# Counting the ones of a graph's adjacency: a column of the attention products against a pass over the stored mask in the second layer

## The chip, the cores and the metric

The kernel runs on one core of one Trainium2 chip. The metric is the device time of one execution in microseconds (us), the median over several executions. TensorE is PE in the profile, its weight loads PEld, VectorE is DVE, ScalarE is ACT, GpSimd is POOL and SyncE, which here only issues DMAs, is SP. L894 is line 894 of the kernel before.

## What is computed

Two graph layers over 8192 nodes with 128 features and a dense 8192 x 8192 adjacency of zeros and ones in float32 (256 MB). Cut to what matters:

```
h = relu(layernorm(x));  Wh = h @ W
e = leaky_relu(Wh @ a1 + (Wh @ a2).T, 0.2)          # 8192 x 8192
att = softmax(where(adj > 0, e, -9e15), axis=1)
x = x + GRU(att @ Wh, h)                            # first layer
h = relu(layernorm(x))
x = x + adj @ (h @ W1.T + b1)                       # second layer
```

The fast path of the kernel is right only if every element of the adjacency is 0 or 1, so it also tests that: for each strip of rows it counts the elements that are not zero and the elements that are exactly one, and if the two counts differ anywhere, a slow general path is run afterwards. With these inputs the counts agree and that path isn't run. The change concerns where the ones are counted.

## The kernel before

**The first layer.** The adjacency is read once, as 128 transposed pieces of 2 MB: 32 blocks of 256 nodes (`NS = 32`, index `g`) times 4 chunks (`CS = 4`, index `c`), each chunk holding 16 groups of 128 neighbours (`JC = 16`). For each piece VectorE writes `Y`, a fp8 mask that is 0.5 where the element equals one (`ones_of`, L617), which SP stores to HBM (`mask_bytes`, 512 KB a piece) for the second layer. The leaky ReLU's two slopes split the mask in two: ScalarE (L469) and VectorE (L672) compute the sign of the edge value for the groups of 128, and VectorE makes the two masks by a bitwise AND (L680) and XOR (L684) into `M`. ScalarE counts the elements that are not zero: a sign of the raw words, summed along the row (`count`, L478, and L556 for four pieces that are counted late).

TensorE then multiplies each mask (the weights, fp8, 128 x 128) with a table `TB` (the moving side, f16), 256 products a block and 8192 in all (`products`, L894). A row of the table has 129 high parts (128 features and the softmax denominator), 129 low parts, and before the change a column of ones, which makes each product 259 columns wide and counts the elements of the mask. ScalarE copies the four sums of a block out (`evacuate`, L490), VectorE adds high and low parts (`attended`, L689) and the two counts (L690, into `cn`), and a GRU and a layer norm follow for the block, spread over the next three blocks' slots. The result of a block is a row of `GS`, the 256 f16 columns (128 high, 128 low) that the second layer multiplies with.

**The second layer.** For each of the 32 strips `t` the whole stored mask of 2 MB is loaded (`y_load`, L313) into one of four buffers: the two `X` buffers and two pieces of the space of `TB`. TensorE makes 128 products of 256 columns a strip (`span`, L977), VectorE adds the two halves and the residual (`finish`, L797 and L802), and SP stores the strip (L320) and loads the next residual (L316). TensorE orders its work as: most of strips 0, 1 and 2 between the last steps of the GRU, then the rest of these three, then strip 3 and on, one after the other (`rest`). `rest(t)` waits for its strip's mask (`q_in`) and for strip t-4 to be finished (`q_o`). SP's loop loads strip t after TensorE is through with strip t-4 (`q_pe`), then waits for `q_o` and stores.

**The late counting.** Four of the 128 pieces are counted only after the last attention product: ScalarE issues their loads into `Z`, two buffers in the space of `M` (L562), and counts each as it lands (L556). VectorE meanwhile runs `examine` (two long reductions over `GS`, L807 and L808, and small ones) and then the `finish` steps. The counts are joined in `tally`, summed over partitions by TensorE (L1023), and the verdict is made in `judge`.

The queues are strictly in order on each engine, and the semaphore `c_cnt` counts ScalarE's counting passes (128 in all before).

Of the kernel before, what the change touches and what calls it, by code (L numbers as in the profile page):

```python
# [5 lines left out]
N = 8192  # L6
F = 128
P = 128
NT = N // P
# [58 lines left out]
def binary_adjacency(nc, sem, redo, xb, adjb, w, wt, a, wiht, whht, b_ih, b_hh, w1t, b1, out):  # L68
    ctx = ExitStack()
    with ctx:  # L70
# [45 lines left out]
        nz = sb("nz", [P, NS, CS])  # L116
        cn = sb("cn", [P, NT])
        den = sb("den", [P, NT])
# [16 lines left out]
        junk = JK[:, 0:JC * RW // 4].bitcast(u8)  # L135
        Mf = M[:, :, :].rearrange("p c k -> p (c k)").bitcast(f32)
        Z = [Mf[:, b * JC * RW:(b + 1) * JC * RW] for b in range(2)]

# [46 lines left out]
        t_p, t_hi, t_lo, t_lop = sem("t_p"), sem("t_hi"), sem("t_lo"), sem("t_lop")  # L185
        t_sc = k_w = sem("t_sc")

        c_in = [sem(f"c_in{b}") for b in range(2)]
# [47 lines left out]
        with nc.Block() as block:  # L236
            @block.sync
            def _(sp):
# [98 lines left out]
                with sp.Fori(1, NS // 4) as k:  # L337
                    for b in range(4):
                        sp.wait_ge(q_pe, k * 4 + b - 3)
                        y_load(k * 4 + b, b)  # L340
                        sp.wait_ge(q_o, k * 4 + b - 3)
                        store(k * 4 + b - 4, b % 2)
                        x1_load(k * 4 + b - 2, b % 2)
# [9 lines left out]
            def _(pool):  # L353
# [13 lines left out]
                for k in range(3):  # L367
                    pool.wait_ge(p_bias, 2 * k + 1)
                    nc.gpsimd.tensor_copy(bpart[k], src[k]).then_inc(p_bias, 1)
                    if k < 2:  # L370
                        pool.wait_ge(p_bias, 2 * k + 2)
                        nc.gpsimd.tensor_tensor(bres[k], src[k], bpart[k], ALU.subtract).then_inc(p_bias, 1)
                pool.wait_ge(b_in, 112)
                nc.gpsimd.memset(TB[:, :, :, 2 * TW:2 * TW + 2], 1.0).then_inc(p_one, 1)

# [17 lines left out]
            def _(act):  # L393
# [57 lines left out]
                def table_high(i):  # L451
                    act.wait_ge(t_p, i + 1)
                    if i == 0:
                        act.wait_ge(p_one, 3)
                    j, m = i // 2 * 8, i % 2
                    nc.scalar.activation(TB[:, j:j + 8, m, 0:TW], PB[i % 2], ACT.Copy).then_inc(t_hi, 1)
# [25 lines left out]
                def evacuate(q):  # L482
                    for t in range(2):
                        if t == 0:
                            act.wait_ge(e_t0, q + 1)
                        else:
                            act.wait_ge(c_pe, (q + 1) * CS)
                        wait(act, d_hp, q)
                        for m in range(2):
                            ins = nc.scalar.activation(AE[:, 2 * t + m, 0:2 * TW + 1], A[t][m][:, 0:2 * TW + 1], ACT.Copy)  # L490
                        ins.then_inc(e_ev[t], 1)
# [59 lines left out]
                for n in range(LATE + 2):  # L551
                    if n >= 2:
                        g, c = late[n - 2]
                        act.wait_ge(c_in[n % 2], (NS * 2 + n // 2) * 16)
                        act.wait_ge(c_cnt, (NS - 1) * EARLY + n - 2)
                        nc.scalar.activation(junk, Z[n % 2].bitcast(u32), ACT.Sign,  # L556
                                             accum_out=nz[:, g:g + 1, c:c + 1].rearrange("p g c -> p (g c)")).then_inc(
                                                 c_cnt, 1)
                        act.wait_ge(c_cnt, (NS - 1) * EARLY + n - 1)
                    if n < LATE:  # L560
                        g, c = late[n]
                        act.dma_start(Z[n % 2], adjb[g * CS + c, :, :]).then_inc(c_in[n % 2], 16)  # L562

            @block.vector
            def _(dve):
# [120 lines left out]
                def attended(q):  # L686
                    for t in range(2):
                        dve.wait_ge(e_ev[t], q + 1)
                    nc.vector.tensor_tensor(AE[:, :, 0:TW], AE[:, :, 0:TW], AE[:, :, TW:2 * TW], ALU.add).then_inc(d_sum, 1)  # L689
                    nc.vector.tensor_tensor(cn[:, bass.ts(q, 2)],  # L690
                                            AE[:, 0:4:2, 2 * TW:2 * TW + 1].rearrange("p t f -> p (t f)"),
                                            AE[:, 1:4:2, 2 * TW:2 * TW + 1].rearrange("p t f -> p (t f)"), ALU.add)
                    dve.wait_ge(d_sum, q + 1)
# [93 lines left out]
                for g in range(NS, NS + 3):  # L787
                    slot(g, g % 2, g // 2)

                def finish(t, u, b, n):  # L790
                    sums = PH2[b][:, :].rearrange("p (t f) -> p t f", f=2 * F)
# [13 lines left out]
                def examine():  # L805
# [3 lines left out]
                    nc.vector.tensor_reduce(bad[:, 2:3], den[:, :], AX.X, ALU.min).then_inc(k_v, 1)  # L809
                    nc.vector.tensor_reduce(odd[:, :, 1:2], cn[:, :].rearrange("p (g t) -> p g t", t=2), AX.X,  # L810
                                            ALU.add).then_inc(k_v, 1)
                    nc.vector.tensor_tensor(bad[:, 5:6], kt[:, 2:3], bad[:, 5:6], ALU.subtract).then_inc(k_v, 1)
                    nc.vector.tensor_tensor(tmp[:, 0, :], wext[:, 2:F + 2], wext[:, 2:F + 2], ALU.mult).then_inc(k_df, 1)
                    dve.wait_ge(k_v, 5)
                    nc.vector.scalar_tensor_tensor(bad[:, 0:1], bad[:, 1:2], -1.0, bad[:, 0:1], ALU.mult,
                                                   ALU.max).then_inc(k_v, 1)

                def tally():
                    dve.wait_ge(c_cnt, NS * CS)
                    nc.vector.tensor_reduce(odd[:, :, 0:1], nz[:, :, :], AX.X, ALU.add).then_inc(k_df, 1)  # L820
                    dve.wait_ge(k_df, 2)
                    nc.vector.scalar_tensor_tensor(odd[:, :, 0:1], odd[:, :, 1:2], -1.0 / MARK, odd[:, :, 0:1], ALU.mult,
                                                   ALU.add).then_inc(k_df, 1)

                def judge():
# [6 lines left out]
                    for n, (at, limit, op) in enumerate(limits):  # L832
                        dve.wait_ge(k_v, 9 + n)
                        nc.vector.scalar_tensor_tensor(bad[:, 7:8], bad[:, at:at + 1], limit, bad[:, 7:8], op,
                                                       ALU.mult).then_inc(k_v, 1)
                    dve.wait_ge(k_v, 14)
                    nc.vector.tensor_scalar(bad[:, 7:8], bad[:, 7:8], 0.5, None, ALU.is_lt).then_inc(k_v, 1)

                examine()
                for b in range(4):  # L840
                    finish(b, b % 2, b, b // 2)
                with dve.Fori(1, NS // 4 - 1) as k:
                    for b in range(4):
                        finish(k * 4 + b, b % 2, b, k * 2 + b // 2)
                tally()
                for t in range(NS - 4, NS):
                    finish(t, t % 2, t % 4, t // 2)
                    if t == NS - 3:
                        judge()
                dve.wait_ge(k_all, 1)  # L850
# [5 lines left out]
            def _(pe):  # L856
# [34 lines left out]
                def products(g, c, t):  # L891
                    for jj in range(JC):
                        for m in range(2):
                            ins = nc.tensor.matmul(A[t][m][:, 0:2 * TW + 1],  # L894
                                                   rows((mask1, mask2)[m](c), jj)[:, t * P:(t + 1) * P],
                                                   TB[:, c * JC + jj, m, 0:2 * TW + 1], start=(c == 0 and jj == 0),
                                                   stop=(c == CS - 1 and jj == JC - 1))
                    return ins
# [55 lines left out]
                def slot(g, u, k):  # L954
                    for c in range(CS):
                        if isinstance(g, int) and g == 0:
                            pe.wait_ge(t_lo, 2 * (c + 1))
                            pe.wait_ge(t_lop, 2 * (c + 1))
                            if c == 0:
                                pe.wait_ge(p_one, 3)  # L960
                        pe.wait_ge(c_m2, g * CS + c + 1)
# [40 lines left out]
                for b in range(3):  # L1002
                    for d in range(2):
                        ins = span(b, b, d, early, NT)
                    ins.then_inc(q_pe, 1)

                def rest(t, b, n):
                    pe.wait_ge(q_in[b], (n + 1) * 16)
                    wait(pe, q_o, t - 3)
                    pe.sem_inc(turn, 1)  # L1010
                    for d in range(2):
                        ins = span(t, b, d, 0, NT)
                    ins.then_inc(q_pe, 1)

# [4 lines left out]
                for t in range(NS - 4, NS):  # L1019
                    rest(t, t % 4, t // 4)  # L1020
                    if t == NS - 4:
                        pe.wait_ge(k_df, 3)
                        nc.tensor.matmul(GP[:, 0:NS], ones[:, :], odd[:, :, 0:1].rearrange("p g o -> p (g o)"), start=True,  # L1023
                                         stop=True)
                        nc.tensor.matmul(GP[:, P:2 * P], ones[:, :], tmp[:, 0, :], start=True, stop=True).then_inc(k_w, 1)
                pe.wait_ge(k_v, 15)
                nc.tensor.matmul(TG[0:1, 0:1], bad[:, 7:8], ones[:, 0:1], start=True, stop=True).then_inc(k_all, 1)
# [660 lines left out]
```

## Time and profile before

| | |
|---|---|
| median of 3 runs | 1615.08 us (1614.78 to 1615.68) |
| the profiled execution, own time | 1614.28 us |
| its span, first to last instruction | 1612.7 us |
| mean granted TensorE clock over the span | 0.984 |
| PE busy | 1536.0 us (95%) |
| DVE busy | 1138.4 us (71%) |
| ACT busy | 1065.8 us (66%) |
| PE products of the first layer, L894 | 8192, from 70 us to 1152 us |
| PE products of the second layer, L977 | 4096, from 1152 us to 1604 us |

Each engine's busy time is a share of the whole span, but the kernel has two long stages that load the engines differently. In the first layer PE, DVE and ACT are all busy over 95% of the time; in the second, from about 1222 us, DVE runs under 1 us in each 14 us and ACT nothing at all. The 1.6 us between the span and the execution's own time are start and end.

### The profile page before, as it was taken

The page shows a single profiled execution, that of the slowest core. Times are in us where ns is not written, and L with a number is a line of the kernel's source. Part 1 is how long each engine was busy: PE and PEld are TensorE (multiplying, and loading weights), DVE is VectorE, ACT ScalarE, POOL GpSimd, SP SyncE. Part 2 cuts the span into 40 slices and gives each one's busy share as a digit, 9 for nine tenths or more (in the row PEclk, how much of TensorE's full clock was granted, in tenths as well). Part 3 has the DMA queues.
Part 4 walks back from the last instruction along what each step waited for, and adds up shares of the span by engine and source line. Part 5 has one row for each costly group of instructions (what it writes and reads, how often), then busy time and mean ns, then how long its engine had stood idle before and what let it go on. Part 6 is the DMA issues. An engine that isn't in the chain of part 4 may idle for free.

```text
span 1612.7 us, 34927 instructions
## 1 busy us (share of the span) xinstructions
PE 1536.0 (95%) x13260; PEld 1335.1 (83%) x13260; DVE 1138.4 (71%) x2290; ACT 1065.8 (66%) x1805; POOL 44.5 (3%) x59
## 2 busy tenths in 40 slices
PE   5448999999999999999999999999999999999997
PEld 5336888888888888888888888888888888888887
DVE  8799999999999999999999999999250000000001
ACT  5669999999999999999999999999121000000000
POOL 0220000000000000000000000000000000000000
PEclk9779999999999999999999999999999999999999
DMA  8649999999999999999999999997558444444430
GB/s 330 237 153 348 340 341 338 339 345 336 339 343 339 340 337 344 340 344 338 340 344 341 343 331 341 342 337 283 212 214 357 174 162 159 161 165 176 176 124 15
DMA packets 79955, 454.16 MB, mean 282 GB/s; under 512 B 9176, under 2 KB 38434, under 8 KB 58914
## 3 DMA queue, kind: packets, MB, share of 16 engines
q1 hardware_dynamic: 78322, 444.54, 74.6%
q10 hardware_dynamic: 1584, 8.98, 1.4%
q8 instruction: 28, 0.46, 0.1%
q14 instruction: 21, 0.17, 0.0%
HBM read 369.57 MB, written 83.92 MB: 281 GB/s over the span
## 4 chain that ended last, share of the span: by engine, by line
PE 92%; DVE 5%; DMA 1%; issue 1%; ACT 0%; DVEq 0%; ACTq 0%
PE A L894 56%; PE A L977 28%; PE GP L918 3%; PE GP L919 2%; DMA h_columns<-AE 1%; PE GQ L937 1%; DVE AE L653 1%; PE GP L920 1%; PE GP L917 1%; DVE M L672 1%; DVE JK L653 1%; DVE Y L617 1%; PE TG L904 0%; PE TG L926 0%; DVE JK L569 0%
## 5 line engine op out<-in xcount | busy, mean ns | idle before, releaser
L894 PE MATMUL A<-TB,M 128*128 128x259 f16 x8192 | 940.8, 275 | 47.1 <-DVE M L684 41.1
L894 PEld LDWEIGHTS A<-TB,M 128*128 128x128 fp8e4 x8192 | 797.4, 97 | 174.0 <-issue 48.3
L469 ACT ACTIVATE M<-SB,dsteep 128x256 fp8e4<-128x256 f32 x1164 | 477.5, 502 | 0.0
L478 ACT ACTIVATE JK<-X 128x4096 uint8<-128x4096 uint32 x124 | 448.0, 3613 | 0.0
L617 DVE TENSOR_SCALAR Y<-X 128x4096 fp8e4<-128x4096 f32 x128 | 292.7, 2287 | 3.8 <-DMA X<-in_adjb_dram 3.7
L797 DVE SCALAR_TENSOR_TENSOR hp<-A,R 128x256 f32<-128x256 f32 x32 | 13.6, 425 | 367.5 <-PE A L977 349.0
L672 DVE TENSOR_SCALAR M<-SB,nd 128x256 fp8e4<-128x256 f32 x884 | 250.2, 355 | 0.0
L977 PE MATMUL A<-WG,X 128*128 128x256 f16 x2048 | 225.7, 273 | 0.0
L977 PE MATMUL A<-WG,TB 128*128 128x256 f16 x2048 | 225.2, 273 | 0.0
L977 PEld LDWEIGHTS A<-WG,TB 128*128 128x128 fp8e4 x2048 | 200.4, 98 | 23.2
L977 PEld LDWEIGHTS A<-WG,X 128*128 128x128 fp8e4 x2048 | 200.4, 98 | 23.1
L684 DVE TENSOR_TENSOR M<-Y,M 128x1024 uint32<-128x1024 uint32 x128 | 156.8, 1225 | 4.4
L680 DVE TENSOR_TENSOR M<-M,Y 128x1024 uint32<-128x1024 uint32 x128 | 155.9, 1218 | 0.5 <-issue 0.4
L490 ACT ACTIVATE AE<-A 128x259 f32<-128x259 f32 x128 | 42.0, 383 | 43.3 <-PE A L894 43.3
L918 PE MATMUL GP<-wihT,hpT 128*128 128x384 f32 x128 | 51.7, 486 | 0.0
L386 POOL TENSOR_TENSOR rstd<-ve,half 128x2 f32<-128x2 f32 x32 | 22.9, 716 | 1041.8 <-DVE ve L741 1041.8
L919 PEld LDWEIGHTS GP<-whhT,R 128*128 128x128 f32 x128 | 24.3, 190 | 17.0
L919 PE MATMUL GP<-whhT,R 128*128 128x256 f32 x128 | 38.1, 379 | 0.0
L689 DVE TENSOR_TENSOR AE<-AE 128x516 f32<-128x516 f32 x32 | 22.4, 699 | 21.8 <-ACT AE L490 21.6
L920 PEld LDWEIGHTS GP<-whhT,R 128*128 128x128 f32 x128 | 24.3, 190 | 3.3
L918 PEld LDWEIGHTS GP<-wihT,hpT 128*128 128x128 f32 x128 | 24.3, 190 | 2.4
L556 ACT ACTIVATE JK<-M 128x4096 uint8<-128x4096 uint32 x4 | 14.5, 3617 | 17.9 <-DMA M<-in_adjb_dram 17.9
(133 smaller groups left out, 696.8 us busy)
## 6 DMA issues: line engine op xcount, KB each, us to landing
X<-in_adjb_dram SPq DMA_DIRECT2D x128, 2048.0 KB, 9.5
mask_bytes<-Y SPq DMA_DIRECT2D x128, 512.0 KB, 4.7
X<-mask_bytes SPq DMA_DIRECT2D x16, 2048.0 KB, 9.3
TB<-mask_bytes SPq DMA_DIRECT2D x16, 2048.0 KB, 9.2
M<-in_adjb_dram ACTq DMA_DIRECT2D x4, 2048.0 KB, 10.2
M<-in_xb_dram SPq DMA_DIRECT2D x8, 512.0 KB, 8.5
h_rows<-M SPq DMA_DIRECT2D x8, 512.0 KB, 6.6
R<-in_xb_dram SPq DMA_DIRECT2D x32, 128.0 KB, 6.8
```

The costliest lines, as they stand in the source:

```text
L469: ins = nc.scalar.activation(rows(mask1(c), jj), SB[u][:, :], ACT.Sigmoid, scale=STEEP, bias=dsteep[:, j:j + 1], saturate=False)
L478: nc.scalar.activation(junk, X[c % 2][:, :].bitcast(u32), ACT.Sign, accum_out=nz[:, bass.ts(g, 1), c:c + 1].rearrange("p g c -> p (g c)")) ...
L490: ins = nc.scalar.activation(AE[:, 2 * t + m, 0:2 * TW + 1], A[t][m][:, 0:2 * TW + 1], ACT.Copy)
L617: nc.vector.tensor_scalar(Y[c % 2][:, :].bitcast(f8), X[c % 2][:, :], 1.0, MARK, ALU.is_equal, ALU.mult, saturate=False).then_inc(c_y, 1)
L672: ins = nc.vector.tensor_scalar(rows(mask1(c), jj), SB[u][:, :], nd[:, j:j + 1], None, ALU.is_ge, saturate=False)
L680: nc.vector.tensor_tensor(mask1(c), mask1(c), Y[c % 2][:, :], ALU.bitwise_and).then_inc(c_m1, 1)
L684: nc.vector.tensor_tensor(mask2(c), Y[c % 2][:, :], mask1(c), ALU.bitwise_xor).then_inc(c_m2, 1)
L894: ins = nc.tensor.matmul(A[t][m][:, 0:2 * TW + 1], rows((mask1, mask2)[m](c), jj)[:, t * P:(t + 1) * P], TB[:, c * JC + jj, m, 0:2 * TW + ...
L918: nc.tensor.matmul(bank[:, 0:3 * F], a_t, wihT[:, :], start=False, stop=False)
L919: nc.tensor.matmul(bank[:, 0:2 * F], h_t, whhT[:, 0:2 * F], start=False, stop=False)
L920: ins = nc.tensor.matmul(bank[:, 3 * F:4 * F], h_t, whhT[:, 2 * F:3 * F], start=False, stop=True)
L977: ins = nc.tensor.matmul(PH2[b][:, d * 2 * F:(d + 1) * 2 * F], YB[b][:, j * RW + d * P:j * RW + (d + 1) * P], GS[:, j, :], start=(d == 0 a ...
```

## The change

The table's rows lose the column of ones: the 8192 attention products are 258 columns wide, the copies out of PSUM too, and the addition into `cn` is gone, as is GpSimd's writing of the ones. The ones are counted from the stored mask in the second layer: for each strip VectorE adds the two halves of the 16384 fp8 values of a partition into 8192 (`halved`), and ScalarE sums these with its accumulator into `cy`. The halves lie in the space of `M` that the late loads (`Z`) use, so the first `halved` waits for all 128 counting passes. `halved(t)` stands ahead of `finish(t)` in VectorE's queue. Since the mask buffer of a strip is now also read by VectorE, SP loads strip t after `q_o` of strip t-4, not after `q_pe`. `tally`, `judge` and TensorE's small sums move to the last strip.

```diff
-        cn = sb("cn", [P, NT])
+        cy = sb("cy", [P, NS])
+        halves = [Mf[:, b * N // 4:(b + 1) * N // 4].bitcast(f8) for b in range(2)]
+        junk8 = Mf[:, N // 2:3 * N // 4].bitcast(u8)
...
                 with sp.Fori(1, NS // 4) as k:
                     for b in range(4):
-                        sp.wait_ge(q_pe, k * 4 + b - 3)
+                        sp.wait_ge(q_o, k * 4 + b - 3)
                         y_load(k * 4 + b, b)
-                        sp.wait_ge(q_o, k * 4 + b - 3)
                         store(k * 4 + b - 4, b % 2)
                         x1_load(k * 4 + b - 2, b % 2)
...
-                            ins = nc.scalar.activation(AE[:, 2 * t + m, 0:2 * TW + 1], A[t][m][:, 0:2 * TW + 1], ACT.Copy)
+                            ins = nc.scalar.activation(AE[:, 2 * t + m, 0:2 * TW], A[t][m][:, 0:2 * TW], ACT.Copy)
...
+                for t in range(NS):
+                    act.wait_ge(q_half, 16 + t + 1)
+                    act.wait_ge(c_cnt, NS * CS + t)
+                    nc.scalar.activation(junk8, halves[t % 2], ACT.Copy, accum_out=cy[:, t:t + 1]).then_inc(c_cnt, 1)
...
-                    nc.vector.tensor_tensor(cn[:, bass.ts(q, 2)],
...
+                def halved(t, b, n):
+                    dve.wait_ge(q_in[b], (n + 1) * 16)
+                    dve.wait_ge(c_cnt, NS * CS + (max(t - 1, 0) if isinstance(t, int) else t - 1))
+                    dve.sem_inc(turn, 1)
+                    nc.vector.tensor_tensor(halves[b % 2], YB[b][:, 0:N], YB[b][:, N:2 * N], ALU.add,
+                                            saturate=False).then_inc(q_half, 1)
...
                 examine()
                 for b in range(4):
+                    halved(b, b, 0)
                     finish(b, b % 2, b, b // 2)
                 with dve.Fori(1, NS // 4 - 1) as k:
                     for b in range(4):
+                        halved(k * 4 + b, b, k)
                         finish(k * 4 + b, b % 2, b, k * 2 + b // 2)
+                halved(NS - 4, 0, NS // 4 - 1)
+                for t in range(NS - 4, NS - 1):
+                    halved(t + 1, t % 4 + 1, NS // 4 - 1)
+                    finish(t, t % 2, t % 4, t // 2)
                 tally()
-                for t in range(NS - 4, NS):
-                    finish(t, t % 2, t % 4, t // 2)
-                    if t == NS - 3:
-                        judge()
+                judge()
+                finish(NS - 1, 1, 3, (NS - 1) // 2)
...
-                            ins = nc.tensor.matmul(A[t][m][:, 0:2 * TW + 1],
+                            ins = nc.tensor.matmul(A[t][m][:, 0:2 * TW],
                                                    rows((mask1, mask2)[m](c), jj)[:, t * P:(t + 1) * P],
-                                                   TB[:, c * JC + jj, m, 0:2 * TW + 1], start=(c == 0 and jj == 0),
+                                                   TB[:, c * JC + jj, m, 0:2 * TW], start=(c == 0 and jj == 0),
```

VectorE's queue at the start of the second layer, from the end of `examine` on, before the change. A00 to A11 are the PSUM banks of strips 0 to 3, R holds the residual and the result.

```order
L815 SCALAR_TENSOR_TENSOR bad<-bad 128x1 [waits k_v]
L797 SCALAR_TENSOR_TENSOR hp<-A00,R 128x256 [waits q_x0,q_pe]
L802 SCALAR_TENSOR_TENSOR R<-A00,hp 128x256 [waits q_lo]
L797 SCALAR_TENSOR_TENSOR hp<-A01,R 128x256 [waits q_x1,q_o,q_pe]
L802 SCALAR_TENSOR_TENSOR R<-A01,hp 128x256 [waits q_lo]
```

The same place after the change.

```order
L822 SCALAR_TENSOR_TENSOR bad<-bad 128x1 [waits k_v]
L796 TENSOR_TENSOR M<-X0 128x8192 [waits q_in0,c_cnt]
L806 SCALAR_TENSOR_TENSOR hp<-A00,R 128x256 [waits q_x0,q_pe]
L811 SCALAR_TENSOR_TENSOR R<-A00,hp 128x256 [waits q_lo]
L796 TENSOR_TENSOR M<-X1 128x8192 [waits q_in1,c_cnt]
L806 SCALAR_TENSOR_TENSOR hp<-A01,R 128x256 [waits q_x1,q_o,q_pe]
L811 SCALAR_TENSOR_TENSOR R<-A01,hp 128x256 [waits q_lo]
```

A pass over the strip's mask that waits for `c_cnt` now stands ahead of each pair of `finish` instructions.

SP's queue at the first turn of the second layer's loop, before the change. X0 receives strip 4, X1 strip 5.

```order
L313 ISA [waits q_pe]
L313 DMA X0<-mask_bytes 128x4096
L320 ISA [waits q_o]
L320 DMA out_0_dram<-R 128x256
L316 ISA
L316 DMA R<-x_after_gat 128x256
L313 ISA [waits q_pe]
L313 DMA X1<-mask_bytes 128x4096
```

The same place after the change.

```order
L316 ISA [waits q_o]
L316 DMA X0<-mask_bytes 128x4096
L323 ISA
L323 DMA out_0_dram<-R 128x256
L319 ISA
L319 DMA R<-x_after_gat 128x256
L316 ISA [waits q_o]
L316 DMA X1<-mask_bytes 128x4096
```

The load of a strip's mask stands behind the wait for `q_o`, which `finish` raises, where it stood behind TensorE's `q_pe`.

## Rows read from the trace of the kernel before

**Rows 1.** The page: busy time and share of each engine; the chain.

```profile
PE 1536.0 (95%) x13260; PEld 1335.1 (83%) x13260; DVE 1138.4 (71%) x2290; ACT 1065.8 (66%) x1805; POOL 44.5 (3%) x59
...
PE 92%; DVE 5%; DMA 1%; issue 1%; ACT 0%; DVEq 0%; ACTq 0%
PE A L894 56%; PE A L977 28%; PE GP L918 3%; PE GP L919 2%; DMA h_columns<-AE 1%; PE GQ L937 1%; DVE AE L653 1%; PE GP L920 1%; PE GP L917 1%; DVE M L672 1%; DVE JK L653 1%; DVE Y L617 1%; PE TG L904 0%; PE TG L926 0%; DVE JK L569 0%
```

**Rows 2.** The chain in order of time, first layer: start us, us, what.

```profile
416.08 7.16 PE A L894 x64
...
423.91 14.32 PE A L894 x128
```

**Rows 3.** The same view, second layer.

```profile
1188.53 373.57 PE A L977 x3422
...
1562.54 41.93 PE A L977 x384
```

**Rows 4.** The same view, before the first layer: f32 products of 130 columns.

```profile
20.20 0.89 PE A L867 x8
```

**Rows 5.** Waits in 60:160 us: who <- whom, total, times, longest.

```profile
PE A L894 <- DVE M L684: 41.1, 4, 18.7
...
PE A L894 <- issue: 6.0, 1, 6.0
```

**Rows 6.** Windows: busy us (instructions) of each engine, PEclk, DMA share, GB/s.

```profile
400.00:800.00 400.00, 400.00 (x3423) 344.21 (x3422) 387.41 (x760) 385.35 (x647) 8.68 (x12) 1.00 0.92 340
```

**Rows 7.** Waits in 400:800 us, 12.2 blocks.

```profile
ACT AE L490 <- PE A L894: 14.7, 12, 1.2
DVE AE L689 <- ACT AE L490: 5.4, 10, 0.6
```

**Rows 8.** Groups by line and form: busy us, mean ns, idle before.

```profile
L478 ACT ACTIVATE JK<-X 128x4096 uint8<-128x4096 uint32 x124 | 448.0, 3613 | 0.0
L617 DVE TENSOR_SCALAR Y<-X 128x4096 fp8e4<-128x4096 f32 x128 | 292.7, 2287 | 3.8 <-DMA X<-in_adjb_dram 3.7
...
L684 DVE TENSOR_TENSOR M<-Y,M 128x1024 uint32<-128x1024 uint32 x128 | 156.8, 1225 | 4.4
...
L690 DVE TENSOR_TENSOR cn<-AE 128x2 f32 x26 | 4.0, 154 | 0.0
...
L807 DVE TENSOR_REDUCE bad<-WG 128x1 f32<-128x8192 f16 x1 | 8.7, 8677 | 0.0
```

**Rows 9.** Timeline around the late counting: start us, us, instruction.

```profile
1196.34 0.34 SPq L313 DMA_DIRECT2D X<-mask_bytes  x1
...
1201.18 0.34 ACTq L562 DMA_DIRECT2D M<-in_adjb_dram  x1
...
1207.10 0.42 DVE L797 SCALAR_TENSOR_TENSOR hp<-A,R 128x256 f32<-128x256 f32 x1
1207.55 0.42 DVE L802 SCALAR_TENSOR_TENSOR R<-A,hp 128x256 f32<-128x256 f32 x1
...
1208.16 0.36 SPq L320 DMA_DIRECT2D out_dram<-R  x1
...
1208.53 0.33 ACTq L562 DMA_DIRECT2D M<-in_adjb_dram  x1
...
1212.18 3.62 ACT L556 ACTIVATE JK<-M 128x4096 uint8<-128x4096 uint32 x1 [3.68 <-DMA M<-in_adjb_dram]
...
1212.49 27.94 PEld L977 LDWEIGHTS A<-WG,X 128*128 128x128 fp8e4 x256
...
1217.93 3.62 ACT L556 ACTIVATE JK<-M 128x4096 uint8<-128x4096 uint32 x1 [2.04 <-DMA M<-in_adjb_dram]
```

**Rows 10.** The page: DMA issues, KB each, median us to landing.

```profile
X<-mask_bytes SPq DMA_DIRECT2D x16, 2048.0 KB, 9.3
```

**Rows 11.** The chain in order of time: 64 products after a wait of PE.

```profile
120.03 9.57 PE A L894 x64
135.57 8.66 PE A L894 x64
```

**Rows 12.** Windows over the same two stretches.

```profile
120.00:129.40 9.40, 9.37 (x64) 0.75 0.86 293
135.50:144.00 8.50, 8.43 (x64) 0.83 0.98 379
```

More of the change, by code:

```diff
@@ L186, in binary_adjacency @@
         t_sc = k_w = sem("t_sc")
+        q_half = t_p
         c_in = [sem(f"c_in{b}") for b in range(2)]
@@ L372, in _ @@
                         nc.gpsimd.tensor_tensor(bres[k], src[k], bpart[k], ALU.subtract).then_inc(p_bias, 1)
-                pool.wait_ge(b_in, 112)
-                nc.gpsimd.memset(TB[:, :, :, 2 * TW:2 * TW + 2], 1.0).then_inc(p_one, 1)
                 for i in range(1, 16, 2):
@@ L453, in table_high @@
                     if i == 0:
-                        act.wait_ge(p_one, 3)
+                        act.wait_ge(b_in, 112)
                     j, m = i // 2 * 8, i % 2
@@ L689, in attended @@
                     nc.vector.tensor_tensor(AE[:, :, 0:TW], AE[:, :, 0:TW], AE[:, :, TW:2 * TW], ALU.add).then_inc(d_sum, 1)
-                    nc.vector.tensor_tensor(cn[:, bass.ts(q, 2)],
-                                            AE[:, 0:4:2, 2 * TW:2 * TW + 1].rearrange("p t f -> p (t f)"),
-                                            AE[:, 1:4:2, 2 * TW:2 * TW + 1].rearrange("p t f -> p (t f)"), ALU.add)
                     dve.wait_ge(d_sum, q + 1)
@@ L809, in examine @@
                     nc.vector.tensor_reduce(bad[:, 2:3], den[:, :], AX.X, ALU.min).then_inc(k_v, 1)
-                    nc.vector.tensor_reduce(odd[:, :, 1:2], cn[:, :].rearrange("p (g t) -> p g t", t=2), AX.X,
-                                            ALU.add).then_inc(k_v, 1)
                     nc.vector.tensor_tensor(bad[:, 5:6], kt[:, 2:3], bad[:, 5:6], ALU.subtract).then_inc(k_v, 1)
                     nc.vector.tensor_tensor(tmp[:, 0, :], wext[:, 2:F + 2], wext[:, 2:F + 2], ALU.mult).then_inc(k_df, 1)
-                    dve.wait_ge(k_v, 5)
+                    dve.wait_ge(k_v, 4)
                     nc.vector.scalar_tensor_tensor(bad[:, 0:1], bad[:, 1:2], -1.0, bad[:, 0:1], ALU.mult,
@@ L818, in tally @@
                 def tally():
-                    dve.wait_ge(c_cnt, NS * CS)
+                    dve.wait_ge(c_cnt, NS * CS + NS)
                     nc.vector.tensor_reduce(odd[:, :, 0:1], nz[:, :, :], AX.X, ALU.add).then_inc(k_df, 1)
                     dve.wait_ge(k_df, 2)
-                    nc.vector.scalar_tensor_tensor(odd[:, :, 0:1], odd[:, :, 1:2], -1.0 / MARK, odd[:, :, 0:1], ALU.mult,
+                    nc.vector.scalar_tensor_tensor(odd[:, :, 0:1], cy[:, :].rearrange("p (g o) -> p g o", o=1), -1.0 / MARK, odd[:, :, 0:1], ALU.mult,
                                                    ALU.add).then_inc(k_df, 1)
@@ L832, in judge @@
                     for n, (at, limit, op) in enumerate(limits):
-                        dve.wait_ge(k_v, 9 + n)
+                        dve.wait_ge(k_v, 8 + n)
                         nc.vector.scalar_tensor_tensor(bad[:, 7:8], bad[:, at:at + 1], limit, bad[:, 7:8], op,
                                                        ALU.mult).then_inc(k_v, 1)
-                    dve.wait_ge(k_v, 14)
+                    dve.wait_ge(k_v, 13)
                     nc.vector.tensor_scalar(bad[:, 7:8], bad[:, 7:8], 0.5, None, ALU.is_lt).then_inc(k_v, 1)
@@ L958, in slot @@
                             pe.wait_ge(t_lop, 2 * (c + 1))
-                            if c == 0:
-                                pe.wait_ge(p_one, 3)
                         pe.wait_ge(c_m2, g * CS + c + 1)
@@ L1005, in _, with sums @@
                     ins.then_inc(q_pe, 1)
+                def sums():
+                    pe.wait_ge(k_df, 3)
+                    nc.tensor.matmul(GP[:, 0:NS], ones[:, :], odd[:, :, 0:1].rearrange("p g o -> p (g o)"), start=True,
+                                     stop=True)
+                    nc.tensor.matmul(GP[:, P:2 * P], ones[:, :], tmp[:, 0, :], start=True, stop=True).then_inc(k_w, 1)
                 def rest(t, b, n):
@@ L1012, in rest @@
                         ins = span(t, b, d, 0, NT)
+                        if d == 0 and isinstance(t, int) and t == NS - 1:
+                            sums()
                     ins.then_inc(q_pe, 1)
@@ L1020, in _ @@
                     rest(t, t % 4, t // 4)
[L1021 to L1026, printed above, removed]
+                pe.wait_ge(k_v, 14)
                 nc.tensor.matmul(TG[0:1, 0:1], bad[:, 7:8], ones[:, 0:1], start=True, stop=True).then_inc(k_all, 1)
```

## The prediction

> **What bounds the kernel now.** I read the page first: PE is busy 95% of the span and holds 92% of the chain that ended last, 56% in the attention products and 28% in the products of the second layer [rows 1]. Shares over the whole span hide the stages, so I read the chain in order of time next. In the first layer 64 attention products take 7.16 us and 128 take 14.32 us, 111.9 ns each, with nothing between them [rows 2]. In the second layer 3422 products take 373.57 us and 384 take 41.93 us, 109.2 ns each [rows 3]. Both stages are bound by the pace of TensorE's products, and it is that pace which the change touches in the one and leaves alone in the other.
>
> The pace isn't proportional to the columns: 259 columns cost 2.7 ns more than 256, or 0.9 ns a column, where a column at 2.4 GHz is 0.42 ns. So the number of columns alone doesn't say what one of them is worth, and that is the first unknown of the sum.
>
> How much faster may TensorE get before another engine is the bound? In 400:800 us, 12.2 blocks of 32.8 us, DVE is busy for 387.4 us and ACT for 385.4 us [rows 6]. Per block ACT waits 14.7/12 = 1.2 us for PE's last sum, and DVE waits 5.4/12 = 0.45 us for ACT's copy of it [rows 7]; these waits are the slack. DVE also loses the count's addition, 0.15 us a block [rows 8], so TensorE can gain about 0.6 us a block (2.3 ns a product) before VectorE stops it.
>
> **What the narrower products give.** Five groups of 64 products at the start wait for masks (four times 41.1 us for DVE, once 6.0 us at issue) [rows 5]; what is saved in them is waited away. That leaves 8192 - 320 = 7872 products. The bounds: nothing, if 258 columns go at the pace of 259; and at most 2.7 ns, the pace of 256, or 21 us. A column of clock, 0.42 ns, gives 3.3 us; the slope of the rows, 0.9 ns, gives 7.1 us. One more row bears on it: f32 products of 130 columns take 0.89/8 = 111 ns [rows 4], about what 259 columns of f16 take, and their moving side has 520 bytes a row against 518. It speaks for a cost that follows the bytes in steps, but not for the size of the step: from 518 to 516 bytes may be a step or none. I take the slope, 7.1 us, since it lies between the two readings of the step. It is 0.23 us a block, inside the slack of 0.6 us.
>
> The Trainium skill (TensorE: Matmul & The Clock Gate, Back-to-back issue gap) gives the gap of products as the columns over 2.4 GHz plus about 2.5 ns. That is 109.2 ns for 256 columns, where this trace agrees, but 110.4 ns for 259, where it measures 111.9; for 258 it gives 110.0, which would save 1.9 ns a product from today's pace, 15 us in all.
>
> **What the counting costs.** The pass `halved` is a two-operand VectorE instruction of 8192 fp8 elements, which the trace lacks. Nearest rows: the reduction over 8192 f16 takes 8.68 us; the AND of 1024 words 1.225 us, at whose rate 8192 would take 9.8 us; and the one-operand `ones_of` does 4096 in 2.29 us, whose rate would give 4.6 us [rows 8]. I take 8.7 us, the row with the same number of elements, and keep 4.6 and 9.8. ScalarE's sum of 8192 is twice its 4096, 7.2 us [rows 8]. In the steady second layer TensorE takes 128 x 109.2 = 14.0 us a strip, VectorE needs 8.7 + 0.9, ScalarE 7.2: both fit beside it and cost nothing there. Without that cover, a strip would take what VectorE takes.
>
> **Where it isn't covered: the first turn.** VectorE's queue now has `halved(0)` ahead of `finish(0)`, and it waits for the last of the four late counts. Before, only `tally` waited for these, some 330 us later. The fourth count starts at 1217.93 and ends at 1221.6 [rows 9]. It may come somewhat earlier, since its loads then have no mask load beside them: the third took 11.0 us from issue to count (1201.18 to 1212.18), the fourth 9.4, against 9.3 for a usual 2 MB load [rows 9, 10]. I take 1221.0. Then, on the clock of before:
>
> `halved(0)` ends at 1221.0 + 8.7 = 1229.7. `finish(0)` takes 0.9, and SP issues 0.2 us behind it (L802 ends at 1207.97, the issue is at 1208.16) [rows 9]: 1230.8. What is late next is the mask of strip 4, whose issue was at 1196.34 [rows 9] and is now behind `q_o`. It takes 9.3 us to land [rows 10]: 1240.1. TensorE starts strip 3 at 1212.49 [rows 9] and is through at 1226.5. It has nothing else in its queue, and waits 13.6 us.
>
> The wait has a second price. After the waits at the start 64 products took 9.57 and 8.66 us, not 7.16 [rows 11], with the granted clock at 0.75 and 0.83 over these stretches [rows 12]: for a part of each it stood at 1.2 GHz. That is 1.5 to 2.4 us; I take 2.0.
>
> Does it repeat? VectorE needs 9.6 us a strip from there: `finish` of strips 0 to 3 is done at about 1230.6, 1240.2, 1249.8 and 1259.4, and masks 5, 6 and 7 land 9.5 us later each, at 1249.7, 1259.3 and 1268.9. TensorE ends strips 4, 5 and 6 at 1256.1, 1270.1 and 1284.0 and finds them all. VectorE gains 4.4 us a strip and catches up at strip 7 or 8. So there is one stall.
>
> At the end, the last ScalarE sum is done some 3 us after TensorE begins strip 31, and TensorE asks for it only after half of that strip, 7 us in: nothing. The small sums, GpSimd's missing fill and the narrower copies are off the path: nothing each; the cover is the products' stream, and uncovered they are under 0.5 us.
>
> **The sum.** 13.6 + 2.0 - 7.1 = +8.5 us. On the profiled execution's 1614.3 us that is 1622.8; this execution is 0.8 us under the median, so the median goes to 1623.6. I say 1623.5.
>
> **The rivals.**
> 1. The column was free: 258 columns go at the pace of 259, since the step in bytes lies elsewhere. For it: 130 f32 columns cost the same as 259 f16. Against it: the general slope. The stall stands alone: 1615.1 + 15.6 = 1630.7.
> 2. The column was dear: the excess of 259 over what 256 lead to expect (111.9 less 109.2 less three columns of 0.42, 1.5 ns) goes with the odd column, and with the column's own 0.42 ns 1.9 ns a product are saved, 14.9 us. For it: 259 is the only odd width in the two stages. Against: 130 is even and has about the same pace. 15.6 - 14.9 = +0.7, so 1615.8. The formula of the Trainium skill above (TensorE: Matmul & The Clock Gate, Back-to-back issue gap) leads to the same pace.
> 3. Faster than before: the pace falls to that of 256 columns, 109.2 ns. 21 us saved, though VectorE's slack of 2.3 ns a product stops it near 18 us: 1615.1 + 15.6 - 18 = 1612.7, and with a pass at 4.6 us, which takes 4.1 us from the stall, 1608.6. It decides from 2.0 ns a product on, where the saving pays for the stall. Nothing in the rows says that two columns above 256 are free.
> 4. VectorE becomes the bound of the second layer: if the pass takes over 13.1 us, each strip takes longer than TensorE's 14.0. At twice my price, 17.4 us, it is 18.3 a strip, some 135 us more: 1750. The rate of every two-operand row speaks against it.
>
> **How the numbers follow.** A measurement of this kernel can't tell changes below 0.2% (3.2 us) from none. Chances: my forecast, a pace gain of 0.4 to 1.3 ns, 38%; rival 1 28%; rival 2 22%; rival 3 8%; rival 4 3%; the rest 1%. The stall itself may be 11.5 to 15 us by the landing times, 9.5 if the pass is short. The range goes from rival 2 less a shorter stall, 1613, to rival 1 plus a longer one, 1632; the likeliest case alone spans 1619 to 1628. Faster by over 3.2 us: rival 3 and a little of 2, 9%. Within: most of rival 2 and a little of mine, 21%. Slower: 70%.
>
> **What would show it.** The chain should have 64 attention products in about 7.10 us (7.16: rival 1; 7.04: rival 2; 6.99: rival 3). L796 should have a mean of 8.7 us, and L567 7.2 us. TensorE should have a wait of 13 to 14 us near 1220 to 1235 us that ends with DMA X<-mask_bytes, and then 64 products in 9 us with a lower clock. SP should have its longest wait there for L811. No second wait of TensorE should follow. If there is no such wait, the step on the order of `halved(0)`, `finish(0)` and the mask of strip 4 is wrong; if the pace of the products doesn't move by 0.4 to 1.3 ns, the step on the slope is.

## The result, and the profile after

The changed kernel takes 1635.3 us (median of 4, 1634.96 to 1636.12) against 1615.4 us before: 19.9 us more, ratio 1.0125, 95% interval 1.011 to 1.014. The forecast was slower, by 8.1 us; the sign was right and the size less than half. The profiled execution has a span of 1633.5 us, 20.8 us more than before.

The chain of the changed kernel in order of time (start us, us, what), at the end of the first layer and around the start of strip 4; the lines answer to [rows 2] and [rows 3]. L905, L986, L796, L806, L811 and L567 are now the attention products, the second layer's products, the pass over the mask, the two `finish` instructions and ScalarE's sum.

```profile
1130.33 7.10 PE A L905 x64
...
1138.10 7.10 PE A L905 x64
1145.20 6.33 PE A L986 x58
...
1182.29 13.25 DMA M<-in_adjb_dram
1195.57 3.72 ACT JK L556 x2
1199.31 1.09 DMA M<-in_adjb_dram
1200.40 12.02 issue
1212.41 0.06 DVE M L796
1212.48 8.55 issue
1221.02 0.43 DVE hp L806
...
1231.56 386.23 PE A L986 x3520
```

64 attention products take 7.10 us, not 7.16: 110.96 ns each, 0.9 ns less than before. The second layer begins at 1145.20, where it began at 1151.86: 6.7 us gained. And from 1182 to 1231.6 the chain is no longer TensorE's: it goes over the late counting's loads and counts, the first pass and the first two `finish` steps. The 12.02 us called issue are VectorE's wait for the late counting, whose end the profile doesn't name as the releaser; the timeline below has the last count from 1208.57 to 1212.2.

Who waited for whom from 1140 us on (in total, times, longest):

```profile
DVE hp L806 <- PE A L986: 99.3, 24, 5.4
...
PE A L986 <- DVE R L811: 25.5, 1, 25.5
```

TensorE waits once in the second layer, for 25.5 us; before it never waited there. The windows over this wait, the 13.9 us behind it and the next strip (busy us of PE, PEld, DVE, ACT and POOL, PEclk, DMA share, GB/s):

```profile
1206.10:1231.50 25.40, 0.01 (x1) 0.00 (x0) 19.02 (x7) 11.80 (x5) 0.00 (x0) 0.60 0.26 98
1231.50:1245.40 13.90, 13.84 (x111) 11.68 (x112) 13.87 (x4) 11.63 (x3) 0.00 (x0) 0.86 0.73 256
1245.60:1259.50 13.90, 13.90 (x130) 12.46 (x128) 13.46 (x5) 9.28 (x5) 0.00 (x0) 1.00 0.66 251
```

In the second window TensorE is never idle and yet issues 111 products, where the third has 130: the granted clock is 0.86 on the mean, since a part of it is still at 1.2 GHz after the wait. Two strips take 29.9 us there, and 28.1 us in the kernel before: 1.8 us. So 25.5 + 1.8 - 6.7 = 20.6 us, of 20.8.

The timeline of the changed kernel shows what stands in this wait:

```profile
1190.66 15.45 PE L986 MATMUL A<-WG,TB 128*128 128x256 f16 x140
...
1208.57 3.62 ACT L556 ACTIVATE JK<-M 128x4096 uint8<-128x4096 uint32 x1 [2.69 <-DMA M<-in_adjb_dram]
...
1212.41 8.69 DVE L796 TENSOR_TENSOR M<-X 128x8192 fp8e4<-128x8192 fp8e4 x1 [12.02 <-issue]
1221.02 0.42 DVE L806 SCALAR_TENSOR_TENSOR hp<-A,R 128x256 f32<-128x256 f32 x1
...
1221.48 0.42 DVE L811 SCALAR_TENSOR_TENSOR R<-A,hp 128x256 f32<-128x256 f32 x1
...
1222.07 0.34 SPq L316 DMA_DIRECT2D X<-mask_bytes  x1
...
1231.56 29.91 PE L986 MATMUL A<-WG,X 128*128 128x256 f16 x256 [25.45 <-DVE R L811]
```

The last late count ends at 1212.2, the pass runs to 1221.0, `finish` to 1221.9, the mask of strip 4 is issued at 1222.07 and TensorE goes on 9.5 us later. TensorE itself had been through since 1206.1, at the end of a group of 140 products. The groups of the page that are new:

```profile
L567 ACT ACTIVATE M<-M 128x8192 uint8<-128x8192 fp8e4 x32 | 225.0, 7032 | 173.2 <-DVE M L796 173.2
...
L796 DVE TENSOR_TENSOR M<-X 128x8192 fp8e4<-128x8192 fp8e4 x16 | 138.9, 8687 | 13.5 <-issue 13.5
```

### The profile page after: what moved, and what is told of

Same layout as the page of the kernel before. It is cut to its first block, busy times and chain, and to the rows that moved or that the text cites. A ratio compares the mean times of both kernels' runs of the same rounds, so it can differ in the third digit from the quotient of the medians.

```text
span 1633.5 us, 35056 instructions
## 1 busy us (share of the span) xinstructions
PE 1532.7 (94%) x13260; PEld 1336.6 (82%) x13260; DVE 1411.5 (86%) x2289; ACT 1296.1 (79%) x1869; POOL 49.3 (3%) x58
## 4 chain that ended last, share of the span: by engine, by line
PE 89%; DVE 5%; DMA 2%; issue 2%; ACT 1%; DVEq 0%; ACTq 0%
PE A L905 55%; PE A L986 26%; PE GP L929 3%; PE GP L930 2%; DMA h_columns<-AE 1%; PE GQ L948 1%; DVE AE L658 1%; DMA M<-in_adjb_dram 1%; PE GP L931 1%; PE GP L928 1%; DVE M L677 1%; DVE JK L658 1%; DVE Y L622 1%; DVE M L796 1%; PE TG L915 0%
## 5 line engine op out<-in xcount | busy, mean ns | idle before, releaser
L905 PE MATMUL A<-TB,M 128*128 128x258 f16 x8192 | 935.4, 274 | 46.1 <-DVE M L689 39.1
L905 PEld LDWEIGHTS A<-TB,M 128*128 128x128 fp8e4 x8192 | 797.9, 97 | 167.2 <-issue 47.3
L567 ACT ACTIVATE M<-M 128x8192 uint8<-128x8192 fp8e4 x32 | 225.0, 7032 | 173.2 <-DVE M L796 173.2
L986 PE MATMUL A<-WG,X 128*128 128x256 f16 x2048 | 227.3, 274 | 25.5 <-DVE R L811 25.5
L986 PEld LDWEIGHTS A<-WG,X 128*128 128x128 fp8e4 x2048 | 201.2, 98 | 49.8 <-issue 25.7
L986 PE MATMUL A<-WG,TB 128*128 128x256 f16 x2048 | 225.4, 273 | 0.0
L986 PEld LDWEIGHTS A<-WG,TB 128*128 128x128 fp8e4 x2048 | 200.4, 98 | 23.2
L796 DVE TENSOR_TENSOR M<-X 128x8192 fp8e4<-128x8192 fp8e4 x16 | 138.9, 8687 | 13.5 <-issue 13.5
L796 DVE TENSOR_TENSOR M<-TB 128x8192 fp8e4<-128x8192 fp8e4 x16 | 138.9, 8682 | 0.0
L806 DVE SCALAR_TENSOR_TENSOR hp<-A,R 128x256 f32<-128x256 f32 x32 | 13.5, 423 | 99.3 <-PE A L986 99.3
L490 ACT ACTIVATE AE<-A 128x258 f32<-128x258 f32 x128 | 42.3, 389 | 34.4 <-PE A L905 34.4
L386 POOL TENSOR_TENSOR rstd<-ve,half 128x2 f32<-128x2 f32 x32 | 28.0, 874 | 1030.4 <-DVE ve L743 1030.4
L930 PEld LDWEIGHTS GP<-whhT,R 128*128 128x128 f32 x128 | 24.3, 190 | 17.0
```

Source lines behind the costliest of these rows:

```text
L567: nc.scalar.activation(junk8, halves[t % 2], ACT.Copy, accum_out=cy[:, t:t + 1]).then_inc(c_cnt, 1)
L796: nc.vector.tensor_tensor(halves[b % 2], YB[b][:, 0:N], YB[b][:, N:2 * N], ALU.add, saturate=False).then_inc(q_half, 1)
L905: ins = nc.tensor.matmul(A[t][m][:, 0:2 * TW], rows((mask1, mask2)[m](c), jj)[:, t * P:(t + 1) * P], TB[:, c * JC + jj, m, 0:2 * TW], star ...
L930: nc.tensor.matmul(bank[:, 0:2 * F], h_t, whhT[:, 0:2 * F], start=False, stop=False)
L986: ins = nc.tensor.matmul(PH2[b][:, d * 2 * F:(d + 1) * 2 * F], YB[b][:, j * RW + d * P:j * RW + (d + 1) * P], GS[:, j, :], start=(d == 0 a ...
```

## The experiments

Each run is held against the kernel before, run on the same chip. Diffs are against the changed kernel where nothing else is said.

**Narrow products alone.** The kernel before with 258 columns, and no counting of ones.

```diff
-                            ins = nc.tensor.matmul(A[t][m][:, 0:2 * TW + 1],
+                            ins = nc.tensor.matmul(A[t][m][:, 0:2 * TW],
...
-                    nc.vector.tensor_tensor(cn[:, bass.ts(q, 2)],
```

> The kernel before with 258-column products and no counting of ones at all (the ones are left out, the verdict is made from other numbers of the same shape). Theory (the narrower product is worth 0.9 ns, and the whole loss lies in the one wait of TensorE at the second layer's start): 6.7 us under the kernel before, 1608.7 us, and the second layer as long as before. Rival (a part of the loss lies in the first layer or its hand-over): more than 1610 us.

1608.3 us against 1615.6, ratio 0.9957 (0.9940 to 0.9974), and 64 products take 7.10 us. As the theory has it: the first layer's gain is there in full, and nothing of the loss is: TensorE has no wait in the second layer.

**Wide products again.** The opposite half: all of the change, but 259 columns; the column of ones is filled and copied out again, and not used.

```diff
-                            ins = nc.tensor.matmul(A[t][m][:, 0:2 * TW],
+                            ins = nc.tensor.matmul(A[t][m][:, 0:2 * TW + 1],
```

> The changed kernel with the products again 259 columns wide, the column of ones filled and copied but not used; all else of the change stays. Theory (gain and loss are independent and add up): the pace of 64 products returns to 7.16 us, and the time is 6.7 us over the changed kernel, 1642 us. Rival (the narrowing itself was hidden by something else in the first layer): within 3 us of the changed kernel.

1642.0 us, ratio 1.0162 (1.0145 to 1.0179), 64 products in 7.16 us, TensorE's wait 25.8 us. It is 6.7 us over the changed kernel; gain and loss are independent and add up.

**The pass freed of the late counting.** The halves lie in the unused end of the table's space.

```diff
-        halves = [Mf[:, b * N // 4:(b + 1) * N // 4].bitcast(f8) for b in range(2)]
+        halves = [TBf[:, 16384 + b * 4096:16384 + (b + 1) * 4096].bitcast(f8) for b in range(2)]
...
-                    dve.wait_ge(c_cnt, NS * CS + (max(t - 1, 0) if isinstance(t, int) else t - 1))
+                    if not isinstance(t, int) or t > 1:
+                        dve.wait_ge(c_cnt, NS * CS + t - 1)
```

> The changed kernel with the halves in the unused end of the table's space, so that the first pass doesn't wait for the late counting, VectorE's order unchanged. Theory (TensorE waits for the mask of strip 4, which waits for examine, the first pass and the finish, one after the other): the pass starts 12 us earlier, right behind examine, the wait of TensorE falls from 25.5 to about 13.5 us, 1623.3 us in all. Rival (the loads of the late counting set when the mask of strip 4 lands): the wait falls by less than 6 us, over 1629 us.

1623.4 us, ratio 1.0045 (1.0028 to 1.0061). The timeline of this kernel, with the pass at L797:

```profile
1200.48 8.68 DVE L797 TENSOR_TENSOR TB<-X 128x8192 fp8e4<-128x8192 fp8e4 x1
...
1210.13 0.34 SPq L316 DMA_DIRECT2D X<-mask_bytes  x1
...
1219.53 30.72 PE L987 MATMUL A<-WG,X 128*128 128x256 f16 x255 [13.27 <-DVE R L812]
```

The pass starts 11.9 us earlier, right behind `examine`, and TensorE's wait is 12.2 us shorter (13.3 us). So the wait for the late counting gave 12 us of the loss. The rest, 13.3 us of waiting, is still there with VectorE's order unchanged.

**The pass ahead of `examine`.** As the run before, with four halves and the order changed.

```diff
-                examine()
                 for b in range(4):
                     halved(b, b, 0)
                     finish(b, b % 2, b, b // 2)
+                examine()
```

> As the run with the halves in their own space, with four of them, and with examine moved behind the finish of strip 3, so that the pass over strip 0 is VectorE's first work after the last low_part. Theory (the pass costs nothing beside TensorE's 14.0 us a strip once it starts early enough): no wait of TensorE for strip 4, 1608.7 us, as with no counting. Rival (VectorE or ScalarE beside TensorE cost something in each strip): over 1611 us, and the second layer's strips longer than 13.97 us.

1607.9 us, ratio 0.9950 (0.9933 to 0.9967). The waits from 1140 us on have no line of TensorE, and from 1183.19, in the last of the work done ahead on strip 2, to the middle of strip 31 the chain is one piece of TensorE's:

```profile
1183.19 408.50 PE A L987 x3742
```

That is 109.2 ns a product, as in [rows 3], with VectorE and ScalarE counting beside it. With the ones counted it is as fast as the run that counts none (1608.3). The mask of strip 4 is issued at 1193.63 here. Two things were changed at once, the order and the number of halves, and no run has the new order with two halves; what each gave is not shown.

**Which of two ends TensorE's wait?** In the changed kernel strip 4 starts 9.5 us behind its mask's issue and 0.3 us behind the `finish` of strip 1, because a pass and a `finish` take as long as a mask takes to land. The trace names the second. In the code TensorE waits before strip 4 for its mask and for the `finish` of strip 0 only, which speaks for the first; the run puts them apart.

```diff
-                examine()
                 for b in range(4):
                     halved(b, b, 0)
                     finish(b, b % 2, b, b // 2)
+                    if b == 0:
+                        examine()
```

> The changed kernel with examine (17.6 us of VectorE) moved from ahead of the first pass to between the finish of strip 0 and the pass over strip 1. In the changed kernel TensorE's strip 4 starts at 1231.6 us, both 9.5 us behind the issue of its mask (1222.07) and 0.3 us behind the finish of strip 1, so the two can't be told apart. Theory (it waits for the mask of strip 4 alone): strip 4 still starts near 1231.5, though strip 1 is finished only near 1249; then strip 5 waits for its own mask, issued near 1249 and landed near 1258.5, some 11 us, and the time is about 12 us over the changed kernel, 1647. Rival (it waits for the finish of strip 1): strip 4 starts near 1249.3.

1648.5 us in one execution (1646.7 us of span), 31.9 us over the kernel before on the same chip, which is 12 us more than the changed kernel was over it. The timeline:

```profile
1222.09 0.34 SPq L316 DMA_DIRECT2D X<-mask_bytes  x1
...
1231.38 16.13 PE L987 MATMUL A<-WG,X 128*128 128x256 f16 x128 [25.25 <-DMA X<-mask_bytes]
...
1248.54 0.42 DVE L811 SCALAR_TENSOR_TENSOR R<-A,hp 128x256 f32<-128x256 f32 x1
...
1249.15 0.34 SPq L316 DMA_DIRECT2D X<-mask_bytes  x1
...
1258.46 16.23 PE L987 MATMUL A<-WG,X 128*128 128x256 f16 x128 [10.96 <-DVE R L811]
```

Strip 4 starts at 1231.38 though strip 1 is finished only at 1249: it is the mask. And strip 5 then waits for its own, 11.0 us: it starts 9.3 us behind that mask's issue. The trace names `finish` again, that of strip 2, which the code doesn't let strip 5 wait for. Each of the two strips takes 16.1 to 16.2 us and not 14.0, so the clock's price is paid twice.

**The pace of the products.** Four runs, none of which counts ones, changed one property each of the narrow kernel (258 columns, the table's rows 260 f16 or 520 bytes apart, the two masks' products in turn): the distance of the rows, the width (256 and 260), and the order. The first was executed four times, the other three once each. Their expectations call the cost of the address theory A, that of the columns B and that of the change of PSUM bank C.

```diff
-        TB = sb("TB", [P, NT, 2, TC], f16)
+        TB = sb("TB", [P, NT, 2, 264], f16)
```

> The narrow products with no counting of ones (left out), the table's rows 264 f16 apart (528 bytes, a multiple of 16) and not 260 (520 bytes). The trace so far has 64 products of 258 columns in 7.10 us, 110.96 ns each. Theory A (every second product starts at an address that isn't a multiple of 16, and pays for it): 110.0 ns, 7.04 us for 64, 1601 us in all. Theory B (the cost follows the number of columns alone, 0.9 ns for each above 256): 110.96 ns as before, 1608 us.

1600.6 us, ratio 0.9915 (0.9898 to 0.9932); 64 products take 7.04 us. Theory A's number.

```diff
-                            ins = nc.tensor.matmul(A[t][m][:, 0:2 * TW],
+                            ins = nc.tensor.matmul(A[t][m][:, 0:2 * TW - 2],
```

> 256-column products with the rows 260 apart, no counting of ones; the low parts of the last feature and of the denominator are left out, as is the count. Theory A (address): above the second layer's 109.2 ns, about 110.2. Theory B (columns): 109.2 ns, 6.99 us for 64, 1594 us if VectorE lets it; its slack of 2.3 ns a product from the pace of 259 columns would hold it at about 1597.

1596.2 us and 6.99 us for 64: 109.2 ns although the rows still start alternately at and off a multiple of 16 bytes. Theory A's 110.2 fails here: the start alone isn't what costs. The span is 3.6 us under that of the rows 264 apart, where the pace would give 6.5; VectorE's waits for ScalarE's copy are down to 1.1 us from 140 us on in the first layer, so its slack is nearly used up. Of the other 3 us, 1.5 lie at the start: the fourth group of 64 products starts at 146.09 us here and at 144.61 with the rows 264 apart. Where the rest went was not tested.

```diff
-                            ins = nc.tensor.matmul(A[t][m][:, 0:2 * TW],
+                            ins = nc.tensor.matmul(A[t][m][:, 0:2 * TW + 2],
```

> 260-column products, two columns of ones copied along and not used, no counting. Theory of the slope: 112.7 ns, 7.21 us for 64, 1622 us. Theory of the step in bytes (259 columns cost what 260 do, as the 130 columns of f32 suggested): 111.9 ns, 7.16 us, 1615 us. Theory A (address and an odd column apart): under 111.9 ns, since 260 is even.

1615.2 us and 7.16 us for 64: 260 columns cost what 259 do, as the step in bytes has it. The slope fails, and so does theory A, which had less than 111.9 ns for an even width.

```diff
-                    for jj in range(JC):
-                        for m in range(2):
+                    for m in range(2):
+                        for jj in range(JC):
                             ins = nc.tensor.matmul(A[t][m][:, 0:2 * TW],
```

> 258 columns, rows 260 apart, no counting, and a chunk's 16 products of the one mask ahead of its 16 of the other, so that 16 products in a row write one PSUM bank and start at addresses of one kind. Theory A (address): 16 products at 110.0 ns and 16 at about 112. Theory C (the change of bank from product to product costs it): all at 110.0 ns, 1601 us. Theory B: all at 110.96 ns, 1608 us.

1599.8 us and 7.04 us for 64, all at 110.0 ns, also the sixteen that start 8 bytes off a multiple of 16. It is theory C's number; but with the rows 264 apart the bank changes with every product too, and the pace is 110.0. Neither the start nor the bank costs by itself. A last run, executed once, put the two apart: the order of the run before, so one bank, with starts that alternate within 16 bytes. For the one mask they are at and 8 bytes off a multiple of 16, as expected; for the other they are 12 and 4 bytes off, since 524 isn't a multiple of 8.

```diff
-        TB = sb("TB", [P, NT, 2, TC], f16)
+        TB = sb("TB", [P, NT, 2, 262], f16)
```

> 258 columns, no counting of ones (left out), 16 products of the one mask ahead of 16 of the other, and rows 262 f16 apart, so that products in a row write one PSUM bank but start alternately at and 8 bytes off a multiple of 16. Theory (a change of the start within 16 bytes from product to product is what costs): 110.96 ns, 1608 us. Rival (only with a change of bank as well): 110.0 ns, 1600 us.

1602.2 us and 7.05 us for 64, 110.1 ns. That refutes the theory's 110.96 ns and lies within 0.2 ns of the rival's: at 258 columns the cost appeared only where the start alternated and the bank changed as well.

**Both together.** The early strips with the rows 264 apart, and the kernel before with that distance alone.

> The run with the early strips, the table's rows 264 apart, all ones counted in the second layer. The theory (110.0 ns a product, and the counting hidden) gives 7.7 us under the early strips, 1600.3 us, no slower than the run that counts nothing at this distance (1600.6). Rival (faster products now meet VectorE's or ScalarE's end in the first layer): over 1603 us.

> The kernel before with the one edit of the table's rows 264 apart, the column of ones kept and counted by TensorE, 259 columns. If the extra cost is one of rows that start alternately at and off a multiple of 16 bytes, 110.4 ns a product (109.2 and three columns of 0.42), 7.07 us for 64, 12 us under the kernel before, 1603.5 us; the column of ones is then worth only 3.3 us. If an odd number of columns costs of itself, over 111 ns and over 1608 us.

The first takes 1600.2 us, ratio 0.9903 (0.9888 to 0.9918), and is the fastest that computes and counts everything. The second takes 1606.7 us, ratio 0.9945 (0.9931 to 0.9958). Their chains, 64 products each, in this order:

```profile
703.56 7.04 PE A L906 x64
```

```profile
707.95 7.09 PE A L894 x64
```

259 columns take 110.8 ns at this distance, not 110.4: a miss by about the height of one column, between the two theories.

## Why the prediction was right and wrong

**What bounds the kernel** was right: the pace of TensorE's products sets both stages.

**The narrower product** was right in size: 0.9 ns a product, 7.1 us forecast, 6.7 us measured. Its ground was not. I took the slope between 256 and 259 columns, and the runs show steps: 256, 258, 259 and 260 columns at the distance of 520 bytes take 109.2, 110.96, 111.9 and 111.9 ns. The row of 130 f32 columns [rows 4] had hinted that 518 and 520 bytes cost the same. That 258 lies 0.9 ns below was a guess between two ends, and that it came true was luck. What more there was to gain lay in the distance and the order of the rows, which I didn't look at.

**The price of the pass** was right: 8.69 us against 8.7, ScalarE's sum 7.03 and 0.19 against 7.2, and both hidden in the steady strips, as the early strips and the run without counting show. The chain of the first turn was right in each link: pass, `finish`, SP's issue, landing, each within 0.3 us. The first pass started 1.9 us earlier than I took (1212.4 is 1219.1 on the clock of before). The late loads had no mask load beside them, as I had argued; where two mask loads run beside them again, in the kernel with the early strips, the last two counts start 5.4 and 4.3 us later than in the changed kernel, of which 1.3 us were there before the loads were issued. One stall, no second; the clock's price was 1.8 us for 2.0; the sums at the end cost nothing (TensorE asked for them 3.6 us after they were there).

**The step that failed** is the sentence "TensorE starts strip 3 at 1212.49 [rows 9] and is through at 1226.5". What starts at 1212.49 is strip 4. The row has x256, two strips, and reads X, the buffers of strips 4 and 5; strip 3 reads TB and is inside the group of 140 just before it, 12 products that complete strip 2 and 128 of strip 3. TensorE's rows of the kernel before:

```profile
1194.69 2.78 PE L977 MATMUL A<-WG,X 128*128 128x256 f16 x24
...
1197.32 15.45 PE L977 MATMUL A<-WG,TB 128*128 128x256 f16 x140
...
1212.60 28.11 PE L977 MATMUL A<-WG,X 128*128 128x256 f16 x256
```

So TensorE ran dry at 1212.5 on that clock and not at 1226.5: 14.0 us more of waiting, less the 1.9 us by which the pass started earlier. 13.6 + 14.0 - 1.9 = 25.7, and 25.5 were measured. The term was the wait of TensorE, and it was mis-sized by a whole strip. With 25.5 in its place the sum gives 1615.1 + 25.5 + 2.0 - 7.1 = 1635.5.

My range could not hold it: it took the landing times as the uncertain part of the stall, and the point from which the stall is counted as certain.

**The rivals.** The first three had the right kind (the stall against a pace), with the same wrong stall; their paces, 111.9, 110.0 and 109.2 ns, are none of them the 110.96 that was measured. The one that VectorE becomes the bound is refuted by 8.69 us.

## What to carry to other kernels

Before a stall is priced, find out when the waiting engine runs dry, from the number and the buffers of the group in the timeline and not from the loop's index in the code; an engine with partial work done ahead (three strips nearly complete) may be a whole step further than it seems. A pass that fits beside the bound engine in every turn can still cost more than it saves in the first, if the load of the next turn hangs behind it and it hangs behind old work in its queue or its memory: give it space of its own and put it first. And a product a few columns wider than a round number is worth a trial of the distance and the order of the rows it reads: here 7.6 to 8.9 us for one line.

## What the runs showed of the hardware

- The pace of matmuls with 258 f16 columns, each with its own fp8 weights, was 110.96 ns with rows 520 bytes apart and two masks in turn, 110.0 ns with rows 528 bytes apart, and 110.0 ns with rows 520 apart but 16 products of one mask in a row. 256 columns were at 109.2 ns even with rows 520 apart, 259 at 111.9 (520) and 110.8 (528), 260 at 111.9 (520). The 110.0 ns for 258 columns are what the formula of the Trainium skill gives (TensorE: Matmul & The Clock Gate, Back-to-back issue gap), which it states for isolated products; the 111.9 and 110.8 for 259, where the formula gives 110.4, are not.
- What causes the extra cost stays open. It isn't the start of a row off a multiple of 16 bytes by itself, nor the change of PSUM bank by itself, nor the width alone. A change of the start within 16 bytes from product to product isn't enough either: the run with one bank and rows 524 bytes apart has it and took 110.1 ns. The cost above 110.0 ns at 258 columns was seen only with both changes together, and 256 columns didn't have it with both. Why that is, and why 259 columns take 110.8 ns even with rows 528 bytes apart, where every row starts at a multiple of 16, no run shows.
- A two-operand VectorE instruction over fp8 took 8.69 us for 8192 elements. The one-operand reduction over as many f16 took 8.68 us, and two-operand instructions took 0.42 us for 256 f32 elements and 1.225 us for 1024 of 32 bits; their slope gives about 8.7 us for 8192, an estimate. So the narrow elements gave it no speed.
